# Splitting the low-weight subtraction of a masked graph attention in two halves

## The reference

```python
h = jnp.maximum(_layernorm(x, axis=-1), 0.0)
h1 = h @ a[:d]
h2 = h @ a[d:]
e = jax.nn.leaky_relu(h1 + h2.T, negative_slope=0.01)
attention = jnp.where(adj > 0, e, NEG_BIG)
attention = jax.nn.softmax(attention, axis=1)
return x + attention @ h
```

## Time and profile before

| | us |
|---|---|
| median of three runs | 1597.63 |
| the profiled execution | 1598.51 |
| its span | 1596.6 |
| TensorE busy (matmuls) | 1563.8 |
| VectorE busy | 1490.5 |
| ScalarE busy | 1189.5 |
| GpSimd busy | 382.8 |

### The profile page before, as it was taken

One profiled execution on the slowest core, in us unless ns is written; L12 is line 12 of the kernel. 1 busy time (PEld: TensorE's weight loads), 2 busy tenths in 40 slices (PEclk: granted clock), 3 DMA queues, 4 the chain that ended last, 5 costly groups with the idle time before them and its releaser, 6 DMA issues.

```text
span 1596.6 us, 41402 instructions
## 1 busy us (share of the span) xinstructions
PE 1563.8 (98%) x12950; PEld 1547.3 (97%) x12950; DVE 1490.5 (93%) x2236; ACT 1189.5 (75%) x1240; POOL 382.8 (24%) x487
## 2 busy tenths in 40 slices
PE   5999999999999999999999999999999999999999
PEld 5899999999999999999999999999999999999998
DVE  7899999999999999999999999999999999999998
ACT  7788887777877777767867767767876876876864
POOL 6264234433544321200300400400400400300300
PEclk9999999999999999999999999999999999999999
DMA  6666768777788778867767767767767866766863
GB/s 208 212 195 226 217 201 238 242 237 235 217 246 235 228 223 238 204 188 207 201 188 210 203 187 207 205 186 208 210 184 207 213 184 200 220 183 200 223 176 102
DMA packets 338829, 331.07 MB, mean 207 GB/s; under 512 B 23488, under 2 KB 245696, under 8 KB 338752
## 3 DMA queue, kind: packets, MB, share of 16 engines
q1 hardware_dynamic: 313696, 288.96, 64.0%
q10 hardware_dynamic: 25056, 41.13, 7.7%
HBM read 308.90 MB, written 21.10 MB: 207 GB/s over the span
## 4 chain that ended last, share of the span: by engine, by line
PE 73%; DVE 13%; issue 5%; DMA 2%; POOL 1%; ACT 1%; DVEq 1%; ACTq 0%; POOLq 0%
PE acc L907 24%; PE acc L910 23%; PE acc L909 23%; DVE w_lo L761 7%; DVE W L751 4%; PE T L874 3%; DMA xo<-part_sums 2%; POOL stage L396 1%; DVE T L739 1%; DVE xo L726 0%; ACT w_hi L529 0%; ACT hb L460 0%; DVE adj_in L858 0%; DVEq L748 0%; ACTq L574 0%
## 5 line engine op out<-in xcount | busy, mean ns | idle before, releaser
L907 PE MATMUL acc<-h_hi,w_hi 128*128 128x258 f32 (+1 forms) x4096 | 1182.9, 289 | 14.9 <-DVE w_lo L761 9.4
L910 PE MATMUL acc<-h_hi,w_lo 128*128 128x258 f32 (+1 forms) x4096 | 1154.6, 282 | 0.0
L909 PE MATMUL acc<-h_lo,w_hi 128*128 128x256 f32 (+1 forms) x4096 | 1151.8, 281 | 0.0
L529 ACT ACTIVATE w_hi<-W 128x1024 fp32r<-128x1024 f32 x512 | 541.2, 1059 | 356.2 <-DVE W L751 354.7
L907 PEld LDWEIGHTS acc<-h_hi,w_hi 128*128 128x128 f32 x4096 | 771.8, 188 | 28.6 <-issue 16.1
L751 DVE SCALAR_TENSOR_TENSOR W<-r_rep,g_all,T 128x512 f32<-128x512 f32 (+1 forms) x1024 | 718.9, 744 | 72.6 <-DVE w_lo L761 38.9
L909 PEld LDWEIGHTS acc<-h_lo,w_hi 128*128 128x128 f32 x4096 | 778.6, 190 | 0.0
L910 PEld LDWEIGHTS acc<-h_hi,w_lo 128*128 128x128 f32 x4096 | 774.9, 189 | 0.0
L761 DVE SCALAR_TENSOR_TENSOR w_lo<-W,w_hi 128x1024 fp32r<-128x1024 f32 x512 | 655.2, 1280 | 4.3 <-ACT w_hi L529 3.1
L520 ACT ACTIVATE mask<-adj_in,mhalf 128x2048 fp8e5<-128x2048 int32 x256 | 509.7, 1991 | 8.1 <-DMA adj_in<-in_adj_dram 4.5
L405 POOL TENSOR_TENSOR xb<-xb,stage 128x256 f32<-128x256 f32 x60 | 48.5, 808 | 667.0 <-ACT hb L584 667.0
(11 more groups left out here) (68 smaller groups left out, 251.5 us busy)
## 6 DMA issues: line engine op xcount, KB each, us to landing
adj_in<-in_adj_dram SPq DMA_DIRECT2D x672, 128.0 KB, 2.7
adj_in<-in_adj_dram SPq DMA_DIRECT2D x168, 512.0 KB, 4.3
adj_in<-in_adj_dram SPq DMA_DIRECT2D x64, 768.0 KB, 5.4
adj_in<-in_adj_dram SPq DMA_DIRECT2D x24, 1024.0 KB, 6.5
adj_in<-in_adj_dram SPq DMA_DIRECT2D x256, 64.0 KB, 2.8
part_sums<-stage ACTq DMA_DIRECT2D x24, 516.0 KB, 4.1
xo<-part_sums ACTq DMA_DIRECT2D x24, 516.0 KB, 4.6
r_rep<-r_rows SPq DMA_DIRECT2D x39, 256.0 KB, 4.2
```

The source lines that it names most:

```text
L529: nc.scalar.activation(w_hi[:, k % HL, :], W[:, k % 2, :], ACT.Relu).then_inc(s_hi, 1)
L907: nc.tensor.matmul(acc[:, t, 0:WC], w_hi[:, k % HL, cols], rhs_hi, start=start and u == 0, stop=False)
L909: nc.tensor.matmul(acc[:, t, 0:D], w_hi[:, k % HL, cols], rhs_lo, start=False, stop=False)
L910: last = nc.tensor.matmul(acc[:, t, 0:WC], w_lo[:, k % LL, cols], rhs_hi, start=False, stop=stop and u == 1)
```

## The change

`subtract` makes `w_lo` in two instructions of 512 columns. The first signals a new semaphore, `s_lo0`, the second `s_lo`. In `weights` the wait moves into the loop over u: the first half of `W` waits for `s_lo0`, the second for `s_lo`, both to the value of before. TensorE waits for `s_lo` as before.

```diff
+        s_lo0 = sem("lo_first_half_ready")
         s_lo = sem("lo_ready")
...
-                if wait:
-                    dve.wait_ge(s_lo, g - 1)
                 for u in range(2):
                     e = 2 * (k % 2) + u
+                    if wait:
+                        dve.wait_ge(s_lo if u else s_lo0, g - 1)
                     last = nc.vector.scalar_tensor_tensor(W[:, k % 2, u * BLK:(u + 1) * BLK], r_rep[:, V.v % 2, :],
                                                           g_all[:, ds(G * c + e, 1)], T8[:, k // 2, e, :],
                                                           ALU.max, ALU.mult)
...
-                nc.vector.scalar_tensor_tensor(w_lo[:, k % LL, :], W[:, k % 2, :], 0.0, w_hi[:, k % HL, :].bitcast(f32),
-                                               ALU.max, ALU.subtract).then_inc(s_lo, 1)
+                for u in range(2):
+                    half_pair = slice(u * BLK, (u + 1) * BLK)
+                    nc.vector.scalar_tensor_tensor(w_lo[:, k % LL, half_pair], W[:, k % 2, half_pair], 0.0,
+                                                   w_hi[:, k % HL, half_pair].bitcast(f32),
+                                                   ALU.max, ALU.subtract).then_inc(s_lo if u else s_lo0, 1)
```

## The result

The changed kernel takes 1611.23 us (median of 4 runs, 1610.87 to 1612.56) against 1597.77 us (1597.43 to 1600.85): ratio 1.0081, 95% interval 1.0064 to 1.0099. It is slower by 13.5 us; the forecast was 1596.6 and the range ended at 1607. The profiled execution took 1611.4 us, its span is 13.0 us longer than before.

A forecast was written before the change was run, and what follows sets the result against it. TensorE sets the pace where it can and elsewhere waits for VectorE. Head +0.6, early +3.0 and late -4.6 sum to -1.0 us, giving 1596.6 us from the 1597.6 median; range 1590 to 1607.

The forecast's parts named there:

- the cost of one more start: VectorE's subtraction as two 512-column instructions: 0.60 us each, 1.20 together against 1.13, so +0.07 us per pair.
- eleven subtractions, +0.77: Early stretch from 435.80, where VectorE's loss is TensorE's: 11 subtractions at 0.07 us more each, +0.77 us.
- Rival (a): Beside GpSimd the cut subtraction suffers less: half of the extra 0.4 us gone, three per early stretch, -5, 1591.6 us; chance 0.13.
- +0.37 for starts and waits: One early stretch: +0.77 us for 11 starts, -0.4 back from two subtractions followed directly by `W`.
- the +0.16: By the skill's two rules two halves take 1.38 us where one takes 1.22; not taken, estimated 12 us, 1609.
- Early visits: 200 to 600 us, eight pairs of visits: a loss of +0.37 us in each, +3.0 us in all.
- Late visits: 750 to 1550 us: -4.6 us, including -2.3 for two TensorE stalls (760.16, 766.39) removed in each of seven long visits.
- The head: Head and first full visits, 0 to 200 us: no wait to save, some eight pairs cost 0.07 each, +0.6 us.
- the moved wait: Each half of `W` finds its half of `w_lo` ready; saves 0.18 to 0.33 us per pair without side work, second wait 0.
- (b): A 512-column subtraction start costs what `W`'s does, 0.66 us, another 0.12 per pair: 1613 us; chance 0.12.
- (c): The second wait of `W` isn't free, 0.057 us: +5.0 early, +2.8 late, 1604.4 us; chance 0.14.
- (d): Early stretches stay level because TensorE's lead swallows 0.37 us, the late gain stays: 1593.6 us; chance 0.12.

## Why the prediction was wrong

**The step that failed** is the cost of one more start. It was put at +0.07 us for every pair, "eleven subtractions, +0.77" included. +0.07 is right for a subtraction that meets nobody: from start to start 0.60 us was measured (median of 513), so two take 1.20 against 1.13. But five of the eleven stand beside GpSimd, four of them slower by 0.34 to 0.42 us before the change. There a second start is a second turn, worth up to 0.55 us and not 0.07. The trace of before held the sign of it, subtractions of 1.63 to 1.73 us, and the prediction read it as sharing in time, "which a cut doesn't change". Rival (a) even had the sign the wrong way round. It also counted three such in a stretch. What the ends of GpSimd's and VectorE's instructions show is a wait for a turn, which is paid per instruction. Laying the two timelines side by side before the change would have shown it: 455.62 + 1.09 = 456.71.

The forecast's own stretch of eleven subtractions, in the changed kernel, from its first transpose to its last subtraction:

```profile
445.44 0.33 DVE L740 STREAM_TRANSPOSE T<-mask 128x128 f32<-128x128 f32 x1
445.68 1.55 DVE L764 SCALAR_TENSOR_TENSOR w_lo<-W,w_hi 128x512 fp32r<-128x512 f32 x2
...
464.92 2.15 DVE L764 SCALAR_TENSOR_TENSOR w_lo<-W,w_hi 128x512 fp32r<-128x512 f32 x2
...
468.63 2.12 DVE L764 SCALAR_TENSOR_TENSOR w_lo<-W,w_hi 128x512 fp32r<-128x512 f32 x2
...
478.65 2.25 DVE L764 SCALAR_TENSOR_TENSOR w_lo<-W,w_hi 128x512 fp32r<-128x512 f32 x2
```

It takes 480.90 - 445.44 = 35.46 us, before 469.55 - 435.80 = 33.75: 1.71 more. The excess in it rose from 1.66 to 3.09 us, +1.43; the forecast's +0.37 for starts and waits makes up the rest (1.80 in all, an estimate).

The prediction was right not to take the +0.16 that it worked out from "The DRAIN you can't avoid" in the Trainium skill's "VectorE: DVE Perf Modes", but it quoted that section in part: it goes on that a next operation which isn't held starts earlier. The trace agrees: the second half starts 0.08 us before the first one ends.

**Early visits**: +3.0 forecast, +12.9 measured, about 1.7 in a cycle of 16 pairs. Some 0.3 of it is starts and waits (the forecast's term), the rest the turns: 1.9 us more excess per 16 pairs, of which about 1.4 reach TensorE.

**Late visits**: -4.6 forecast, 0 measured. The gain of the wait is there (VectorE's `W` doesn't wait any more), and the excess of 2.8 us more per 40 pairs stands against it. TensorE's late first matmuls of a pair add up to as much as before: counted where matmuls start over 0.17 us apart, 9.3 us from 750 to 1550 us, and 9.8 in the same stretch, 13 us later, after the change. Others stand in the place of the two stalls that the forecast wanted gone. The run with the change in the late part alone gives 1.0000.

**The head**: +0.6 forecast; TensorE runs 1404 matmuls in the first 200 us against 1405. No difference, within what one matmul is worth; why the +0.6 doesn't show stays open.

**The waits**: the moved wait was right in every part, and its second half costs nothing. Its worth is greater where every pair pays for two starts: 27.1 us.

**The rivals**: the time came out next to (b), 1613, but (b) is refuted: a 512-column subtraction starts 0.60 behind the one before and not 0.66. (c) is refuted by the distance of `W`'s halves (0.66 us as before, not 0.057 more), (d) by the early windows, (a) by the excess, which rose. That the time lies near (b)'s is luck: none of the four was the mechanism that decided. The 1609 by the skill's two rules came near as well, and not by its working: two halves take 1.20 us and not 1.38.

## What to carry to other kernels

Before cutting a VectorE instruction that reads two SBUF tensors, look who else is at work beside it: in this kernel every start beside GpSimd could cost up to 0.55 us, so the number of instructions counted and not only their columns. Where durations of one instruction fall in two groups (here 1.22 and 1.6 to 1.75 us), lay both engines' ends side by side before explaining the slow group. Splitting such an instruction to shorten a wait on one's own last result did harm where the other engine was at work, and none in the pairs that it left alone; that it gains there these runs don't prove (0.9991).

## What the runs showed of the hardware

A subtraction (both tensors in SBUF) and a GpSimd addition or subtraction of 256 columns that overlap take turns: VectorE's ends 0.53 to 0.56 us (512 columns, 158 cases) or 1.07 to 1.09 us (1024 columns, 85 cases) behind GpSimd's end, and a GpSimd instruction that had to wait ends 0.58 to 0.62 us behind VectorE's (0.50 in one line, 405 of the kernel before). `W` (one operand in PSUM; 0.743 us beside GpSimd, 0.746 without), the batch statistics (0.415 in both cases) and the transposes of 256 columns (0.454 and 0.458) are not slowed. VectorE's wait on its own last instruction costs 0.13 to 0.24 us of idle time (middle half of the waits of `W` before the change); behind a wait on the last but one the next instruction starts 0.08 us before the one in front ends, as without a wait.
